# A selective-scan kernel: two PSUM banks for the scan input and two for projection tiles, and a unit's four gates in one go

## The chip, the cores and the metric

The kernel runs on one core of one Trainium2 chip. The metric is the device time of one execution in microseconds (us). One execution was also taken by the hardware profiler; all rows below come from that one.

## What is computed

Two sequences of 1024 tokens with 256 features go through two layers. The first is a state-space layer: a normalisation, then for each direction (forward and backward in time) an input projection, a scan over time, a gate and an output projection, then a gated MLP. The second is attention with 16 heads and a second MLP. The part that the change touches is the scan of the first layer, which for each of 512 channels keeps 64 states:

```python
xs, z = jnp.split(h @ in_w, 2, axis=-1)
xs = jax.nn.silu(xs)
proj = xs @ xproj_w
dt = jax.nn.softplus(proj[..., :D_INNER] + dt_bias)
Bm = proj[..., D_INNER:D_INNER + D_STATE]
Cm = proj[..., D_INNER + D_STATE:]
def step(hst, ins):
    dt_t, B_t, C_t, x_t = ins
    dA = jnp.exp(dt_t[:, :, None] * A)
    hst = hst * dA + (dt_t * x_t)[:, :, None] * B_t[:, None, :]
    y_t = jnp.einsum('bds,bs->bd', hst, C_t)
    return (hst, y_t)
...
y = jnp.swapaxes(ys, 0, 1) + xs * Dskip
return y * jax.nn.silu(z) @ out_w
```

## The kernel before, in words

The scan is cut into 8 units (`UNITS`): direction times sequence times half of the tokens (512). Units 0 to 3 run forward, 4 to 7 backward. In the even units a half starts from zero, in the odd ones it goes on from the end state of the unit before. A unit has 64 state steps (`DS`), numbered st; w counts them through all units, from 0 to 511. Each step has four tiles f = 0 to 3 of 128 channels by 512 tokens, so that there are 2048 scan tiles, numbered n = 4w + f (`U_TILES`).

Every tile goes through five engines' queues, each of which runs in the order in which its program is written; semaphores tie them together.

- ScalarE writes the decay of the tile (`act.activation(decay...)`, L950) and, for the next step, the time-major input scaled by B (`scan_input`, L933). Between steps it does `act_turns`: copies of projection tiles out of PSUM, and in steps 31 and 46 the long silu and softplus operations of the next unit.
- TensorE turns the scaled input into a PSUM bank with four instructions of 128 columns (`turn_u`, L1504 and L1507). I call this the fill of tile n. `take_u` gives the bank, 4 + n % `U_BANKS`, and first waits until the scan that read it last, n - `U_BANKS`, is done. Then, for the same f, TensorE adds the product of step w - 2 onto PSUM banks 0 to 3 (`reduce_state`, L1513, four instructions of 128 columns; `first_state`, with L1533 as well, in a unit's first step). After every odd f it does one piece of a projection for the next unit: `next(pieces, None)` issues one matmul of 512 columns (L1292), or one tile of four transposes. Fill, reduction and the piece if there is one are called a turn here.
- VectorE scans the tile out of the PSUM bank (L1198), 512 tokens in one instruction. After the four tiles of a step it does `dve_turns`. In step 1 of units 1 to 7 it also does `gate_y` (L1181) for the unit before, one gate of 128 by 512 after each of the four scans. A gate waits for the last reduction of the unit before, all four f of it, which TensorE issues in its step 1. TensorE's `first_state(w, c)`, which it issues in its step 2, waits for gate c, since it overwrites that bank.
- GpSimd multiplies the scanned tile by C (L713), two tiles in one instruction.
- SyncE loads the rows of C and the diagonals of B.

The projections are laid out by `turns` and `place_turns`: a tile with two matmuls or one group of transposes takes two steps, a tile with four matmuls three (`PIECES`). Units 1 to 6 have 8 tiles of two matmuls (xs and zs), 7 of four (dt, bc, out) and 9 of transposes (yT, bT, dtxT). Unit 0 has 16 of two (zs of unit 0, mean, sum, xs, zs), 5 of four and 5 of transposes; unit 7 has 14 of two (mean, sum, up), 4 of four and 4 of transposes. `place_tiles` gives each tile of the scan stage the one bank 4 + `U_BANKS`, and `take` makes TensorE wait until the engine that read the tile before it has done so. Before and after the scan the four banks 4 to 7 rotate over all tiles.

Of the kernel before, what the change touches and what calls it, by code (L numbers as in the profile page):

```python
# [42 lines left out]
RECIP_STEPS = (6, 7, 9, 10)  # L43
SUMS_STEP = 4
U_TILES = SCAN_TILES * NI
U_BANKS = 3
DIAGS = 1
DIAG_PAIRS = 3
FILLS = 16
# [8 lines left out]
def build(nc, t):  # L58
# [4 lines left out]
    with ctx:  # L63
# [40 lines left out]
        TB = HALF // P  # L104
# [32 lines left out]

        NORM_AT = {"ln0": (24064, 28160), "ln1": (26112, 22016), "rms0": (26624, 28672), "rms1": (26624, 28672)}
        sq = {name: cut(at, 2, C, HALF) for name, (at, _) in NORM_AT.items()}
        rstd = {name: cut(at, 4, HALF) for name, (_, at) in NORM_AT.items()}  # L140

        mask_i = cut(38912, B, L)[0:1].bitcast(I32)
# [64 lines left out]
        def tiles(name, who):  # L207
            first[name] = len(eaters)
            eaters.extend(who)

        def unit(u):

            d, r = divmod(u, B * HALVES)
            b, hi = divmod(r, HALVES)
            return d, b, hi, (1 - hi if d else hi)
# [59 lines left out]
        def pe_turn(u, st):  # L275
            return TURN[u].get(st)
# [21 lines left out]
        def dve_turns(u, st):  # L298

            step = TURN[u].get(st - 1)  # L300
            todo = [step] if step else []
            if step and step[0] == "mean":
                todo = [("centre",) + step[1:]]
            back = TURN[u].get(st - 2)
            if back and back[0] == "sum":
                todo += steps("recip scale", *back[1:])
            if u == UNITS - 1:
                return todo
            if st == SOFTPLUS_STEP + 1:
                todo.append(("softplus", u + 1))  # L310
            return todo
# [50 lines left out]
        def place_tiles(order, bank_of):  # L362

            for step in order:
                kind, *at = step
                if kind in ("mean", "square") and (at[0], at[1]) not in NEED:
                    NEED[at[0], at[1]] = last_update.get(ORDER[at[0]][at[1]], 0)
                who = {"mods": "d", "mean": "c", "sum": "a", "down": "x", "out": "x", "proj": "x" * C,
                       "xs": "a", "zs": "a", "dt": "a", "bc": "r", "bT": "a", "dtxT": "a", "yT": "a",
                       "qk": "a", "v": "a"}.get(kind, "")  # L370
                if kind == "up":
                    who = "da"[at[2] % 2 == 0]
                tiles(step, who)
                for g in range(len(banks), len(eaters)):
                    banks.append(bank_of(g))
                    before.append(holder.get(banks[g]))
                    holder[banks[g]] = ("tile", g)
                if kind == "out":
                    d, b, hi, half = unit(at[0])
                    last_update[b * HALVES + half] = eaters.count("x")  # L380
                if kind == "down":
                    last_update[ORDER[at[0]][at[1]]] = eaters.count("x")
                if kind == "proj":
                    last_update[at[0]] = eaters.count("x")

        place_tiles(START, lambda g: 4 + g % 4)
        u_before = [holder.get(4 + n) for n in range(U_BANKS)]
        for u in range(UNITS):
            for st in range(DS):
                if pe_turn(u, st):  # L390
                    place_tiles([pe_turn(u, st)], lambda g: 4 + U_BANKS)
        for n in range(U_TILES - U_BANKS, U_TILES):
            holder[4 + n % U_BANKS] = ("u", n)
        place_tiles(LATE, lambda g: 4 + g % 4)
# [9 lines left out]
        def free_bank(pe, was):  # L404

            if was is None:
                return
            kind, n = was
            if kind == "u":
                pe.wait_ge(s["scan_done"], n + 1)  # L410
                return
            name, each = FREES[eaters[n]]
            pe.wait_ge(s[name], each * eaten(n, eaters[n]))
# [6 lines left out]
        def take_u(pe, n):  # L420

            free_bank(pe, u_before[n] if n < U_BANKS else ("u", n - U_BANKS))
            return psum[:, 4 + n % U_BANKS, :]

# [21 lines left out]
        def rows_at(v, m):  # L446


            if m not in ROW_STEPS or (v % 2 and v // 2 + 1 == B * HG):
                return None  # L450
            return 1 - v % 2, (v + 1) // 2, ROW_STEPS.index(m)
# [3 lines left out]
        for v in range(BLOCKS):  # L455
            for m in range(BLOCK):
# [4 lines left out]
                if rows_at(v, m):  # L461
                    half, u, j = rows_at(v, m)
# [30 lines left out]
        def scan_at(w):  # L493

            u, st = divmod(w, DS)
            d, b, hi, half = unit(u)
            if hi:
                return SLIDE if d else 0
            return st // RING if d else SLIDE - st // RING
# [6 lines left out]
        def end_state(w, f):  # L506

            at = scan_at(w) + (0 if unit(w // DS)[0] else HALF - 1)
            return hs[:, w % RING, f, at:at + 1]
# [489 lines left out]
        def _(dve):  # L999
# [133 lines left out]
            def do(order):  # L1133

                for kind, *at in order:
                    if kind == "mods":
                        modulation(*at)
                    if kind == "centre":
                        centre(*at)
                    if kind == "recip":  # L1140
                        recip(*at)
                    if kind == "scale":
                        scale(*at)
                    if kind == "bc":
                        copy_rows(*at)
                    if kind == "softplus":
                        finish_dt(*at)
                    if kind == "decay rate":
                        negate_a()
                    if kind == "out":  # L1150
                        add_output(*at)
                    if kind == "up":
                        gate(*at)
                    if kind == "down":
                        update(*at)
                    if kind == "mask":
                        key_mask()
                    if kind == "rest":
                        rest(*at)
                    if kind == "third part":  # L1160
                        third_part(*at)
                    if kind == "ones of v":
                        ones_of_v(*at)
                    if kind == "first pass":
                        for w in range(*at):
                            score_max(w)
                            if w == SCORE_TILES - 1:
                                finish_max(0)
                    if kind == "proj":
                        add_attention(*at)  # L1170
# [7 lines left out]
            def gate_y(u, c):  # L1178

                dve.wait_ge(s["reduce_done"], NI * (u + 1) * DS)  # L1180
                dve.tensor_tensor(zsT[:, u % 2, c], psum[:, c, :], zsT[:, u % 2, c], ALU.mult)\  # L1181
                   .then_inc(s["gated"], 1)

            for u in range(UNITS):
                d, b, hi, half = unit(u)
                for st in range(DS):
                    w = u * DS + st
                    if hi:
                        dve.wait_ge(s["scan_done"], NI * (w - DS + 1))
                    rows = slice(scan_at(w), scan_at(w) + HALF)  # L1190
                    for f in range(NI):
                        n = NI * w + f
                        if w >= RING:
                            dve.wait_ge(s["reduce_done"], NI * (w - RING) + f + 1)
                        dve.wait_ge(s["decay_ready"], n + 1)
                        dve.wait_ge(s["u_full"], n + 1)
                        way = slice(None, None, -1) if d else slice(None)
                        dve.tensor_tensor_scan(hs[:, w % RING, f, rows][:, way], decay[:, w % 2, f, way],  # L1198
                                               psum[:, 4 + n % U_BANKS, way],
                                               end_state(w - DS, f) if hi else 0.0, op0=ALU.mult, op1=ALU.add)\  # L1200
                           .then_inc(s["scan_done"], 1)
                        if u and st == 1:
                            gate_y(u - 1, f)
                    do(dve_turns(u, st))
            for f in range(NI):
                gate_y(UNITS - 1, f)
# [470 lines left out]
```

## Time and profile before

| | us |
|---|---|
| median of 3 runs | 3551.79 |
| lowest and highest run | 3551.68 and 3552.13 |
| the profiled execution | 3553.52 |
| its span, first to last instruction | 3551.7 |
| mean granted TensorE clock, share of full speed | 0.975 |

The span has a short start (about 67 us), the scan (67.7 to 2726 us), and after it the MLP, the attention and the second MLP. An engine's busy share says how much of the span an instruction of it was running. Matmuls are pipelined and their ends are modelled, so their starts are the firmer numbers; scans on VectorE overlap by some hundredths, so that an interval between starts is shorter than one duration. A row of the timeline merges equal instructions that follow each other with under 0.15 us between them. An idle time in brackets stands with what ended it, which is not always what had caused it.

### The profile page before, as it was taken

How to read it: one execution, taken by the hardware profiler on the slowest of the kernel's cores; microseconds unless marked ns; L12 is line 12 of the kernel's file. 1: busy time of each engine (PE TensorE's matmuls, PEld its weight loads, DVE VectorE, ACT ScalarE, POOL GpSimd, SP SyncE). 2: the span in 40 equal slices, each digit the busy share in tenths (PEclk: the TensorE clock that was granted, in tenths of full speed). 3: DMA queues.
4: the chain of work that ended last, by engine and by line, in shares of the span. 5: the costliest groups of instructions: out<-in, count | busy, mean ns of one | idle time of the engine just before them, and what ended most of it. 6: DMA issues, size and time to landing. Idle time of an engine off the chain costs nothing.

```text
span 3551.7 us, 59805 instructions
## 1 busy us (share of the span) xinstructions
PE 3345.1 (94%) x22946; PEld 2573.6 (72%) x22946; DVE 2983.3 (84%) x2916; ACT 2910.1 (82%) x4664; POOL 2304.6 (65%) x1066
## 2 busy tenths in 40 slices
PE   8998999899989999999999899999899989999999
PEld 5888888888888888988988888888787432222244
DVE  4988999899889989988999899899997488888241
ACT  5999999999998998999999999998896327777621
POOL 1878898898888879888988888798687000000000
PEclk9999999999999999999999999999899989999999
DMA  3222222222222222222222222222111052211000
GB/s 112 72 73 64 79 70 67 61 68 68 68 69 87 66 62 66 70 63 60 79 68 63 60 68 70 59 86 68 51 62 54 17 127 35 37 19 19 1 6 18
DMA packets 192638, 214.17 MB, mean 60 GB/s; under 512 B 75585, under 2 KB 144961, under 8 KB 192097
## 3 DMA queue, kind: packets, MB, share of 16 engines
q1 hardware_dynamic: 192354, 210.36, 20.6%
q8 instruction: 182, 2.98, 0.3%
q14 instruction: 102, 0.84, 0.1%
HBM read 192.19 MB, written 18.06 MB: 59 GB/s over the span
## 4 chain that ended last, share of the span: by engine, by line
PE 67%; ACT 19%; DVE 8%; issue 3%; POOL 2%; DMA 0%; SPq 0%; DVEq 0%; ACTq 0%; POOLq 0%
PE psum L1292 17%; PE psum L1513 16%; PE psum L1507 13%; PE psum L1504 10%; ACT arena L950 8%; ACT arena L933 6%; DVE arena L1198 4%; PE psum L1600 3%; PE psum L1589 3%; PE psum L1564 2%; DVE row_max L1245 2%; POOL arena L697 1%; PE psum L1533 1%; POOL arena L713 1%; ACT L950 1%
## 5 line engine op out<-in xcount | busy, mean ns | idle before, releaser
L1198 DVE TENSOR_TENSOR_SCAN arena<-arena,psum 128x512 f32<-128x512 f32 x2048 | 2379.0, 1229 | 192.1 <-ACT arena L950 105.8
L713 POOL TENSOR_TENSOR arena<-arena 128x1024 f32<-128x1024 f32 x1024 | 2237.5, 2192 | 458.1 <-DVE arena L1198 434.7
L950 ACT ACTIVATE arena<-arena,a_neg 128x512 f32<-128x512 f32 x2048 | 1436.5, 712 | 178.1 <-PE psum L1507 176.3
L1513 PE MATMUL psum<-ident,arena 128*128 128x128 f32 x8192 | 1244.4, 275 | 1.6 <-POOL arena L713 1.6
L933 ACT ACTIVATE arena<-arena,bT 128x512 f32<-128x512 f32 x1536 | 1091.9, 711 | 0.0
L1507 PE MATMUL psum<-ident,arena 128*128 128x128 f32 x6144 | 1021.7, 276 | 0.0
L1513 PEld LDWEIGHTS psum<-ident,arena 128*128 128x128 f32 x8192 | 974.8, 143 | 2.1 <-POOL arena L713 2.1
L1504 PE MATMUL psum<-arena 128*128 128x128 f32 x4096 | 844.5, 288 | 104.4 <-DVE arena L1198 89.8
L1504 PEld LDWEIGHTS psum<-arena 128*128 128x128 f32 x4096 | 656.2, 194 | 350.5 <-issue 185.6
L1507 PEld LDWEIGHTS psum<-ident,arena 128*128 128x128 f32 x6144 | 754.9, 144 | 0.0
L1292 PE MATMUL psum<-arena 128*128 128x512 f32 x1472 | 708.0, 604 | 29.4 <-ACT arena L813 18.3
L1292 PEld LDWEIGHTS psum<-arena 128*128 128x128 f32 x1472 | 257.0, 194 | 221.6 <-issue 192.6
L1245 DVE TENSOR_REDUCE row_max<-psum 128x1 f32<-128x512 f32 x512 | 318.0, 676 | 58.0 <-PE psum L1564 56.6
L985 ACT ACTIVATE arena<-psum 128x512 f32<-128x512 f32 x512 | 273.4, 600 | 82.0 <-PE psum L1589 80.5
L736 POOL TENSOR_TENSOR arena<-skip_w 128x512 f32<-128x512 f32 x16 | 20.3, 1267 | 403.6 <-DVE skip_w L1271 403.6
L1564 PE MATMUL psum<-arena 97*128 97x512 bf16 x512 | 161.4, 393 | 20.3 <-DVE row_max L1245 16.9
L1589 PE MATMUL psum<-arena 100*128 100x512 bf16 x512 | 160.5, 387 | 4.3 <-ACT arena L985 3.2
L1589 PEld LDWEIGHTS psum<-arena 100*128 100x128 bf16 x512 | 35.9, 97 | 158.2 <-ACT arena L985 124.7
L1600 PE MATMUL psum<-arena 128*32 128x512 f32 x1024 | 136.4, 604 | 4.6 <-ACT skip_w L962 4.5
L729 POOL MEMSET arena<- 4x4096 f32 x3 | 10.7, 3579 | 184.5 <-DVE arena L1119 104.9
L1564 PEld LDWEIGHTS psum<-arena 97*128 97x128 bf16 x512 | 50.7, 99 | 100.0 <-DVE row_max L1245 46.3
L891 ACT ACTIVATE arena<-psum,b_up 128x512 f32<-128x512 f32 x32 | 22.0, 687 | 113.4 <-PE psum L1292 113.4
(117 smaller groups left out, 1079.9 us busy)
## 6 DMA issues: line engine op xcount, KB each, us to landing
arena<-bc_dram SPq DMA_DIRECT2D x256, 512.0 KB, 3.7
arena<-diag_dram SPq DMA_DIRECT2D x224, 128.0 KB, 2.1
arena<-qk_dram SPq DMA_DIRECT2D x96, 128.0 KB
diag_dram<-arena SPq DMA_DIRECT2D x32, 256.0 KB, 4.5
qk_dram<-arena SPq DMA_DIRECT2D x12, 512.0 KB, 4.9
arena<-in_x SPq DMA_DIRECT2D x4, 512.0 KB, 10.9
arena<-in_up_w SPq DMA_DIRECT2D x1, 2048.0 KB, 11.7
out_xT<-arena SPq DMA_DIRECT2D x8, 256.0 KB, 2.2
```

Of the source, the lines that this page charges most:

```text
L713: pool.tensor_tensor(out[:, :, way], h_now[:, :, way], c_row, ALU.mult)\
L933: act.activation(uT[:, w % 2, c - DIAGS], dtxT[:, u % 2, c], ACT.Copy, scale=bT[:, u % 2, c, st:st + 1])\
L950: act.activation(decay[:, w % 2, f], dt_[:, u % 2, f], ACT.Exp, scale=a_neg[:, d, f, st:st + 1])\
L985: act.activation(probs[:, w % 4, jj], psum[:, n % 3, :], ACT.Exp)\
L1198: dve.tensor_tensor_scan(hs[:, w % RING, f, rows][:, way], decay[:, w % 2, f, way], psum[:, 4 + n % U_BANKS, way], end_state(w - DS, f) if ...
L1245: dve.tensor_reduce(row_max[:, qt, j, kh:kh + 1], side_bank("scores", w), axis=AX.X, op=ALU.max)\
L1292: o = pe.matmul(dst, lhsT, rhs, start=k == 0, stop=k == len(pairs) - 1)
L1504: o = pe.matmul(dst[:, c * P:(c + 1) * P], dtxT[:, w // DS % 2, c, f * P:(f + 1) * P], diag[:, p % DIAG_PAIRS, w % 2], start=True, stop=True)
L1507: o = pe.transpose(dst[:, c * P:(c + 1) * P], uT[:, w % 2, c - DIAGS, f * P:(f + 1) * P], ident[:, :])
L1513: return pe.matmul(psum[:, c, f * P:(f + 1) * P], hs[:, w % RING, f, at:at + P], ident[:, :], is_transpose=True, start=False, stop=w % DS ...
L1564: pe.matmul(take_side(pe, "scores", w), stack[u % STACKS][0:PLAIN, 0, j, qt * P:(qt + 1) * P], stack[u % STACKS][0:PLAIN, 1, j, tok(kh)], ...
L1589: pe.matmul(psum[:, n % 3, :], stack[u % STACKS][0:ROWS, 1, j, kt * P:(kt + 1) * P], stack[u % STACKS][0:ROWS, 0, j, tok(qh)], start=True, ...
```

## The change

`U_BANKS` goes from 3 to 2, so fill n waits for scan n - 2. The tiles of projections alternate between banks 6 and 7 by their number. The four gates of a unit stand after the four scans of step 1, no longer one after each scan.

```diff
-U_BANKS = 3
+U_BANKS = 2
...
-                    place_tiles([pe_turn(u, st)], lambda g: 4 + U_BANKS)
+                    place_tiles([pe_turn(u, st)], lambda g: 4 + U_BANKS + g % 2)
...
                            .then_inc(s["scan_done"], 1)
-                        if u and st == 1:
-                            gate_y(u - 1, f)
+                    if u and st == 1:
+                        for c in range(TB):
+                            gate_y(u - 1, c)
                     do(dve_turns(u, st))
```

## Rows read from the trace of the kernel before

**Rows 1.** The page: span, busy time by engine, costliest group.
```profile
span 3551.7 us, 59805 instructions
...
PE 3345.1 (94%) x22946; PEld 2573.6 (72%) x22946; DVE 2983.3 (84%) x2916; ACT 2910.1 (82%) x4664; POOL 2304.6 (65%) x1066
...
L1198 DVE TENSOR_TENSOR_SCAN arena<-arena,psum 128x512 f32<-128x512 f32 x2048 | 2379.0, 1229 | 192.1 <-ACT arena L950 105.8
```

**Rows 2.** Busy time by window, unit 2: window, length, busy us, clock.
```profile
740.00:1064.00 324.00, 309.06 (x2457) 280.85 (x2456) 296.02 (x265) 301.50 (x477) 283.62 (x129) 0.98 0.22 67
```

**Rows 3.** Waits of the whole span: waiter, releaser, total us, times, longest.
```profile
PE psum L1292 <- ACT arena L813: 18.3, 7, 4.3
...
DVE arena L1198 <- PE psum L1507: 66.5, 121, 2.4
...
PE psum L1292 <- DVE arena L1034: 3.9, 5, 0.9
```

**Rows 4.** Timeline of VectorE: start, length, instruction, count, idle before.
```profile
910.16 6.93 DVE L1198 TENSOR_TENSOR_SCAN arena<-arena,psum 128x512 f32<-128x512 f32 x6 [4.80 <-ACT arena L950]
...
1504.22 9.12 DVE L1198 TENSOR_TENSOR_SCAN arena<-arena,psum 128x512 f32<-128x512 f32 x8 [0.50 <-ACT arena L950]
1513.84 9.12 DVE L1198 TENSOR_TENSOR_SCAN arena<-arena,psum 128x512 f32<-128x512 f32 x8 [0.50 <-ACT arena L950]
...
1585.99 2.33 DVE L1198 TENSOR_TENSOR_SCAN arena<-arena,psum 128x512 f32<-128x512 f32 x2 [0.50 <-ACT arena L950]
...
1601.27 2.33 DVE L1198 TENSOR_TENSOR_SCAN arena<-arena,psum 128x512 f32<-128x512 f32 x2 [0.50 <-ACT arena L950]
```

**Rows 5.** VectorE without a stop: an even unit, then an odd one.
```profile
1019.29 41.20 DVE L1198 TENSOR_TENSOR_SCAN arena<-arena,psum 128x512 f32<-128x512 f32 x37
...
1373.81 35.10 DVE L1198 TENSOR_TENSOR_SCAN arena<-arena,psum 128x512 f32<-128x512 f32 x30
```

**Rows 6.** TensorE's turns around one projection piece, and the scan behind it.
```profile
804.41 0.39 PE L1504 MATMUL psum<-arena 128*128 128x128 f32 x2
...
805.39 0.39 PE L1504 MATMUL psum<-arena 128*128 128x128 f32 x2
...
807.24 0.39 PE L1504 MATMUL psum<-arena 128*128 128x128 f32 x2
807.47 0.49 PE L1507 MATMUL psum<-ident,arena 128*128 128x128 f32 x3
...
808.09 2.33 DVE L1198 TENSOR_TENSOR_SCAN arena<-arena,psum 128x512 f32<-128x512 f32 x2 [0.50 <-PE psum L1507]
```

**Rows 7.** Steps 60 and 61 of unit 3: scans, and fills that wait for them.
```profile
1383.18 1.25 DVE L1198 TENSOR_TENSOR_SCAN arena<-arena,psum 128x512 f32<-128x512 f32 x1
...
1384.36 1.25 DVE L1198 TENSOR_TENSOR_SCAN arena<-arena,psum 128x512 f32<-128x512 f32 x1
...
1384.49 0.49 PE L1504 MATMUL psum<-arena 128*128 128x128 f32 x2
1384.82 0.49 PE L1507 MATMUL psum<-ident,arena 128*128 128x128 f32 x3
...
1385.66 0.49 PE L1504 MATMUL psum<-arena 128*128 128x128 f32 x2
...
1386.92 0.46 PE L1504 MATMUL psum<-arena 128*128 128x128 f32 x2
```

**Rows 8.** VectorE at unit 4's gates.
```profile
1410.99 0.69 DVE L1181 TENSOR_TENSOR arena<-psum,arena 128x512 f32<-128x512 f32 x1 [2.08 <-PE psum L1513]
...
1416.73 2.32 DVE L1198 TENSOR_TENSOR_SCAN arena<-arena,psum 128x512 f32<-128x512 f32 x2
1419.29 1.22 DVE L1198 TENSOR_TENSOR_SCAN arena<-arena,psum 128x512 f32<-128x512 f32 x1 [0.24 <-PE psum L1507]
1421.17 1.22 DVE L1198 TENSOR_TENSOR_SCAN arena<-arena,psum 128x512 f32<-128x512 f32 x1 [0.66 <-PE psum L1507]
1423.05 1.22 DVE L1198 TENSOR_TENSOR_SCAN arena<-arena,psum 128x512 f32<-128x512 f32 x1 [0.66 <-ACT arena L950]
```

**Rows 9.** Two windows: busy times, then granted clock (third number from the end).
```profile
1375.00:1400.00 25.00, 24.95 (x193) 21.62 (x192) 25.00 (x23) 23.71 (x39) 23.32 (x11) 1.00 0.23 75
...
1413.40:1416.60 3.20, 3.20 (x17) 3.20 (x16) 3.20 (x4) 1.56 (x3) 1.95 (x2) 0.50 0.00 0
```

## The prediction

> **What bounds the kernel now.** I read the page first. TensorE is busy for 94% of the span, but VectorE's scan is the costliest single group: 2048 scans of 1.23 us, 192 us idle before them [rows 1]. A share over the whole span does not say which of the two sets the pace, so I took one unit next. In unit 2's window of 324 us four engines are busy for 309, 296, 302 and 284 us [rows 2]: no engine has much room, and what counts is the order in which they hand tiles over. Then I read the timeline of VectorE beside that of TensorE, which gives two paces.
>
> VectorE's own pace, where it never stops, is 41.20 / 37 = 1.11 us a tile in an even unit and 35.10 / 30 = 1.17 us in an odd one [rows 5]. TensorE's turn without a projection piece is 0.98 us (from fill to fill), and with one matmul of 512 columns 1.85 us [rows 6]. So TensorE is faster than VectorE by 0.13 to 0.19 us in a plain turn and slower by 0.68 to 0.74 us in a turn with a piece. Where a tile of two matmuls lies on eight turns, TensorE needs 6 x 0.98 + 2 x 1.85 = 9.6 us, and VectorE shows exactly that: groups of 8 scans start 9.62 us apart with 0.50 us idle between them [rows 4], whatever releaser the rows name. Where four matmuls lie on twelve turns, it needs 8 x 0.98 + 4 x 1.85 = 15.2 us, and the trace has 15.28 [rows 4]. So most of a unit runs at TensorE's mean pace, and TensorE does not wait in it. What makes that possible is the ring of three banks: in the plain turns TensorE gets ahead by up to three tiles, and a late turn is paid from this lead. Where no pieces are left, TensorE runs into the ring's end: a fill starts 0.05 to 0.06 us after scan n - 3 has ended (1383.18 + 1.25 = 1384.43, then 1384.49; 1384.36 + 1.25 = 1385.61, then 1385.66). The fill of 1384.49 is done at 1385.31, and its scan is due only two scans after 1384.36, at 1386.70: 1.39 us in hand [rows 7].
>
> **Part 1, the ring of two.** It adds a wait: fill n for scan n - 2 in place of n - 3. What is queued behind it on TensorE is the reduction of the same turn, the piece and the next fill; who waits for those is VectorE, and for the reductions nobody soon. I work out whether VectorE then stands still. Let E be the end of scan n - 2. The fill starts at E + 0.06 and, having waited, takes 0.82 us (1384.49 to 1385.31) [rows 7], against 0.72 when it follows without a stop (807.24 to 807.96); the scan starts 0.13 to 0.14 after the fill (807.96 to 808.09) [rows 6]. That is E + 1.02. Scan n is due at E + 1.17 - 0.08 = E + 1.09 in an odd unit (the 0.08 is the overlap of two scans, 1384.43 less 1384.36 [rows 7]) and at E + 1.03 in an even one. So plain turns still hide the fill, by 0.07 and 0.01 us. For f = 0 the fill starts 0.14 after the scan's end (1386.92 against 1385.61 + 1.17 [rows 7]), which makes 1.08: hidden in an odd unit, 0.05 late in an even one, and some 0.08 with the restart. Over about 25 such tiles of an even unit, 2 us.
>
> A piece is no longer hidden. After fill n (at E + 0.06) the next fill comes 1.85 + 0.10 later, and its scan can start 0.72 + 0.14 after it: E + 2.87. It is due at E + 2 x 1.17 - 0.08 = E + 2.26 in an odd unit, E + 2.14 in an even one. VectorE stands for 0.61 or 0.73 us. The next piece comes two turns on: scans then are 0.98 + 1.85 = 2.83 apart, where two scans take 2.34 or 2.22, so each further piece of the run costs 0.50 or 0.62. The time between tiles' runs can't pay for it, since there VectorE sets the pace and a ring of two holds no lead. Hence:
>
> - two matmuls on 8 turns: 8 x 1.17 + 0.61 + 0.50 = 10.47 (odd) and 8 x 1.11 + 0.73 + 0.62 = 10.23 (even), against 9.62: +0.85 and +0.61;
> - four on 12 turns: 14.04 + 0.61 + 3 x 0.50 = 16.15 and 13.32 + 0.73 + 3 x 0.62 = 15.91, against 15.28: +0.87 and +0.63;
> - a tile of transposes: four instructions of 128 columns are half a plain turn, 0.49 us, so a scan that can start at E + 0.06 + 1.08 + 0.49 + 0.86 = E + 2.49: +0.23 and +0.35, all of it hidden now.
>
> The long silu and softplus operations stop VectorE as before (4.80 us before the scan at 910.16 [rows 4]). ScalarE's program is held to TensorE's fills, which now run up to one tile nearer to the scans, so such a stall can grow by 0 to 1.17 us; the fills before it were 0.5 us ahead at most, and I take 0.5 a unit.
>
> **Part 2, the second bank for projections.** It removes the wait of a projection tile for its predecessor's reader. In the trace hardly anything waits for that: the 18.3 us in 7 waits are for L813, the silu of the next unit's gate, whose data the bc tile needs anyway [rows 3]; of the waits for VectorE's centring 3.9 us in all are for the bank or the start [rows 3]. I take 2 us of gain in all, the bounds are 0 and 22 us. The Trainium skill's page Perfetto Trace Analysis, section Matmuls, says that independent matmul groups should rotate through banks so that reading one out overlaps the next. By that rule this half is a gain of up to those 22 us, and the trace shows that one bank already overlaps, since a tile's two or three steps leave its reader time.
>
> **Part 3, the gates in one go.** Now VectorE stops 2.08 us before the first gate with three scans of its own step behind it in its queue, and 0.24, 0.66 and 0.66 us in the next steps [rows 8]: 3.6 us. Afterwards the four scans run first, and by their end the last reduction is in, so the first gate has no wait. What is late next is step 2: TensorE's turn with `first_state` is 1.88 us (1419.29 to 1421.17 [rows 8]) and starts only when gate 0 is done; three turns come 0.46, 0.7 and 0.7 late, 1.9 us. That saves 1.7 us where the trace shows 3.6 and nothing where it is 2; I take 1.0 for each of 7 boundaries, bounds 0 and 3.6. It moves no DMA, and no other engine's queue changes.
>
> **The sum.** Units 1, 3, 5: 8 x 0.85 + 7 x 0.87 + 8 x 0.23 + 0.5 - 1.0 = 14.2 us each (the ninth tile of transposes lies in the softplus stall). Units 2, 4, 6: 8 x 0.61 + 7 x 0.63 + 8 x 0.35 + 2 + 0.5 - 1.0 = 13.6 each. Unit 0: 16 x 0.61 + 5 x 0.63 + 4 x 0.35 + 2, less 2 for pieces that lie in ScalarE's long stretches: 14.3. Unit 7: 14 x 0.85 + 4 x 0.87 + 4 x 0.23 - 1, less 1: 14.3. Together 43 + 41 + 29 = 112, less 2 for part 2: +110 us. The profiled execution took 3553.5 us with a span of 3551.7, the median of the runs is 3551.8; the span and the median agree, and I add to that: 3662 us. Nothing outside the scan changes: after it banks 4 to 7 rotate as before.
>
> **The rivals.**
>
> A: *half price.* If the pieces' stalls are shorter, because fills after a wait catch up by more than the 0.98 us turn shows or waits overlap the copies' turns, +50 us: 3602. For it: the ends of matmuls are modelled, and a fill may in truth be done sooner. Against it: 808.09 less 807.24 = 0.85 holds without the modelled end. 12 in 100.
>
> B: *the ring's loop is longer than a scan.* The plain turns have only 0.01 to 0.07 us to spare. If the loop scan, fill, scan is 0.05 us longer than read, nearly all of the 2048 tiles pay, about 0.04 each: +80 on top, 3740. For it: no row shows a fill and a scan of neighbouring tiles in such close order. Against it: each leg is read from rows. 14 in 100.
>
> C: *not slower.* TensorE is the laggard in most of the scan, so its fills could start after scan n - 2 has ended in any case, and then the third bank is idle; VectorE waits for fills only 66.5 us in all now [rows 3]. The gates would then give back up to 7 x 3.6 = 25 us and part 2 some: 3525. It decides if the fills next to pieces start later than E + 0.06 anyway. Against it: at 9.62 us for 8 tiles TensorE has no idle time, so it can keep that pace only if its six plain turns follow each other at 0.98, faster than scans end. 4 in 100.
>
> D: *the clock.* After TensorE had stopped at unit 4's gates its granted clock was 0.50, which is 1.2 GHz of 2.4 [rows 9]. If many short waits did the same, a plain turn would take twice 0.98, 0.8 more than a scan; over a tenth of the tiles that is +160 us on top, 3825. Against it: in 1375 to 1400 each fill waits for a scan and the clock is 1.00 [rows 9]. The Trainium skill, page TensorE: Matmul & The Clock Gate, section on psum-queue depth-cycling, describes such an oscillation where TensorE pauses often between groups; by that rule this change is at risk, and the row speaks against it here. 2 in 100.
>
> **The numbers.** The forecast, 3662, has 68 in 100, by itself from 3635 to 3700: the pieces' stalls could be 0.1 us off each way (some 350 pieces, 35 us) and the gates 7 to 15 us. Then A 12, B 14, C 4, D 2. The range reaches down to A and up to B: 3600 to 3740. About 0.2%, 7 us, is what a measurement of this kernel can tell from no change. Slower by more: all but C and a little of A, 0.95. Within 0.2%: 0.02. Faster: 0.03.
>
> **What would show it.** In the profile after: TensorE waits for a scan before most plain fills, VectorE's idle time before L1198 (192 us now [rows 1]) grows by about 110 us; groups of 8 scans come 10.2 to 10.5 us apart, not 9.6; four gates follow each other with no idle before the first; scans without pieces keep 1.11 and 1.17 us. If these last ones are longer, B is right. If fills start late after a scan's end although nothing is in front of them, or the groups stay at 9.6, the argument is wrong.

## The result, and the profile after

| | us |
|---|---|
| before, median of 4 runs (3551.3 to 3552.13) | 3551.73 |
| after, median of 4 runs (3676.51 to 3677.6) | 3676.95 |
| ratio, 95% interval | 1.0353, 1.0336 to 1.0369 |
| span of the profiled execution after | 3674.7 |
| mean granted TensorE clock after | 0.976 |

The change makes the kernel slower by 125 us, where 110 were forecast. The span grew by 123.0 us, and all of it lies inside the scan: its first scan starts 67.8 us after the start (before 67.7), and it ends at 2850.4 us (before 2727.4). From one unit's first scan to the next one's, units 0 to 7 are longer by 11.9, 16.0, 16.8, 17.9, 15.4, 17.7, 16.9 and 10.1 us.

The page of the kernel after: engines, then the scan, with its busy us, mean ns and idle us before it (before: [rows 1]). In this kernel the lines from the scan on carry a number higher by 0 or 1 (fill L1505 and L1508, reduction L1514, piece L1293; the gate is L1181 and the scan L1198 in both).

```profile
PE 3466.6 (94%) x22946; PEld 2591.4 (71%) x22946; DVE 3010.2 (82%) x2916; ACT 2929.7 (80%) x4664; POOL 2304.6 (63%) x1066
...
L1198 DVE TENSOR_TENSOR_SCAN arena<-arena,psum 128x512 f32<-128x512 f32 x2048 | 2404.4, 1234 | 301.5 <-PE psum L1508 161.7
```

VectorE stands before its scans for 301.5 us in place of 192.1, and the scans' busy time grew by another 25 us: scans that follow each other overlap by 0.08 us, and a scan after a stop has no such overlap. TensorE's busy time also grew, by 122 us with the same number of instructions, so that the page shows 94% both times: that share says nothing of the change.

The waits of the kernel after (waiter, releaser, total us, times, longest; before: [rows 3]):

```profile
PEld psum L1505 <- DVE arena L1198: 210.7, 464, 7.2
...
DVE arena L1198 <- PE psum L1508: 161.7, 302, 1.7
...
PE psum L1505 <- DVE arena L1198: 107.3, 58, 6.9
...
PE psum L1293 <- ACT arena L813: 13.0, 7, 3.5
```

Fills waited for scans for 195.2 us in 195 cases before (weight loads and matmuls together) and do so for 318.0 in 522 cases now. VectorE's waits for fills went from 66.5 us in 121 cases to 161.7 in 302. Most of these waits are short: 1181 of the 2048 fills start within 0.2 us of the end of the scan whose bank they take, before the change 335. The two engines now wait for each other in turn, which is what a ring that is too short looks like.

The timeline of VectorE in unit 2 (even), first where tiles of two matmuls lie, then tiles of four (start, length, instruction, count, idle before; before: [rows 4]):

```profile
870.51 6.85 DVE L1198 TENSOR_TENSOR_SCAN arena<-arena,psum 128x512 f32<-128x512 f32 x6 [0.50 <-ACT arena L950]
877.92 2.33 DVE L1198 TENSOR_TENSOR_SCAN arena<-arena,psum 128x512 f32<-128x512 f32 x2 [0.56 <-PE psum L1508]
880.76 6.85 DVE L1198 TENSOR_TENSOR_SCAN arena<-arena,psum 128x512 f32<-128x512 f32 x6 [0.50 <-ACT arena L950]
...
959.35 6.85 DVE L1198 TENSOR_TENSOR_SCAN arena<-arena,psum 128x512 f32<-128x512 f32 x6
966.76 2.33 DVE L1198 TENSOR_TENSOR_SCAN arena<-arena,psum 128x512 f32<-128x512 f32 x2 [0.56 <-PE psum L1508]
...
975.26 6.85 DVE L1198 TENSOR_TENSOR_SCAN arena<-arena,psum 128x512 f32<-128x512 f32 x6 [0.50 <-ACT arena L950]
```

A group of eight scans takes 880.76 - 870.51 = 10.25 us (forecast 10.23, before 9.62), one of twelve 975.26 - 959.35 = 15.91 (forecast 15.91, before 15.28). Each piece now shows as a stop of its own, 0.56 for a tile's first and 0.50 for the next. In unit 3 (odd) the same groups are:

```profile
1234.38 7.14 DVE L1198 TENSOR_TENSOR_SCAN arena<-arena,psum 128x512 f32<-128x512 f32 x6 [0.38 <-PE psum L1508]
...
1244.86 7.15 DVE L1198 TENSOR_TENSOR_SCAN arena<-arena,psum 128x512 f32<-128x512 f32 x6 [0.38 <-PE psum L1508]
...
1304.15 7.13 DVE L1198 TENSOR_TENSOR_SCAN arena<-arena,psum 128x512 f32<-128x512 f32 x6
...
1320.29 7.14 DVE L1198 TENSOR_TENSOR_SCAN arena<-arena,psum 128x512 f32<-128x512 f32 x6 [0.38 <-PE psum L1508]
```

That is 10.48 and 16.14 us (forecast 10.47 and 16.15). The Trainium skill, page Perfetto Trace Analysis, section Optimization Strategy, says that the same gap repeating on the engine that should be saturated can mean that there is not enough PSUM to allocate the next tile. The rows after agree. But the kernel before shows gaps of 0.50 us too [rows 4], and those come from TensorE's own work, as its turns show [rows 6]: the gap alone does not tell the two apart, the length of the group beside the sum of TensorE's turns does.

### The profile page after: what moved, and what is told of

It is laid out like the page before. It is cut to its first block, busy times and chain, and to the rows that moved or that the text cites. A ratio compares the mean times of both kernels' runs of the same rounds, so it can differ in the third digit from the quotient of the medians.

```text
span 3674.7 us, 59805 instructions
## 1 busy us (share of the span) xinstructions
PE 3466.6 (94%) x22946; PEld 2591.4 (71%) x22946; DVE 3010.2 (82%) x2916; ACT 2929.7 (80%) x4664; POOL 2304.6 (63%) x1066
## 4 chain that ended last, share of the span: by engine, by line
PE 72%; DVE 13%; ACT 9%; issue 3%; POOL 2%; DMA 0%; SPq 0%; DVEq 0%; ACTq 0%; POOLq 0%
PE psum L1514 17%; PE psum L1293 17%; PE psum L1508 14%; PE psum L1505 13%; DVE arena L1198 9%; PE psum L1601 3%; ACT arena L950 3%; PE psum L1590 3%; ACT arena L933 2%; PE psum L1565 2%; DVE row_max L1246 2%; POOL arena L697 1%; PE psum L1534 1%; POOL arena L713 1%; ACT L950 1%
## 5 line engine op out<-in xcount | busy, mean ns | idle before, releaser
L1198 DVE TENSOR_TENSOR_SCAN arena<-arena,psum 128x512 f32<-128x512 f32 x2048 | 2404.4, 1234 | 301.5 <-PE psum L1508 161.7
L1514 PE MATMUL psum<-ident,arena 128*128 128x128 f32 x8192 | 1244.4, 275 | 0.7 <-POOL arena L713 0.7
L1508 PE MATMUL psum<-ident,arena 128*128 128x128 f32 x6144 | 1021.2, 276 | 0.0
L1505 PE MATMUL psum<-arena 128*128 128x128 f32 x4096 | 908.5, 304 | 118.1 <-DVE arena L1198 107.3
L1505 PEld LDWEIGHTS psum<-arena 128*128 128x128 f32 x4096 | 651.3, 192 | 468.6 <-issue 214.5
L1514 PEld LDWEIGHTS psum<-ident,arena 128*128 128x128 f32 x8192 | 974.8, 143 | 0.9 <-POOL arena L713 0.9
L1508 PEld LDWEIGHTS psum<-ident,arena 128*128 128x128 f32 x6144 | 753.8, 143 | 0.0
L1293 PE MATMUL psum<-arena 128*128 128x512 f32 x1472 | 708.5, 604 | 23.1 <-ACT arena L813 13.0
L1293 PEld LDWEIGHTS psum<-arena 128*128 128x128 f32 x1472 | 257.9, 194 | 214.0 <-issue 191.4
L729 POOL MEMSET arena<- 4x4096 f32 x3 | 10.7, 3578 | 184.6 <-DVE arena L1119 104.8
```

The costliest lines, as they stand in the source:

```text
L1293: o = pe.matmul(dst, lhsT, rhs, start=k == 0, stop=k == len(pairs) - 1)
L1505: o = pe.matmul(dst[:, c * P:(c + 1) * P], dtxT[:, w // DS % 2, c, f * P:(f + 1) * P], diag[:, p % DIAG_PAIRS, w % 2], start=True, stop=True)
L1508: o = pe.transpose(dst[:, c * P:(c + 1) * P], uT[:, w % 2, c - DIAGS, f * P:(f + 1) * P], ident[:, :])
L1514: return pe.matmul(psum[:, c, f * P:(f + 1) * P], hs[:, w % RING, f, at:at + P], ident[:, :], is_transpose=True, start=False, stop=w % DS ...
```

## Experiments

The theory is the forecast's: the ring of two costs what TensorE's plain turns (0.98 us, faster than a scan) could bank before, and the pieces spend it. Each kernel was timed together with the kernel before on the same chip, and that one's median was 3552.4 for e1 to e4, 3552.6 for e5 to e8 and 3553.3 for e9 and e10.

**The gates alone.** The kernel before, its three banks kept, with part 3:

```diff
                             .then_inc(s["scan_done"], 1)
-                        if u and st == 1:
-                            gate_y(u - 1, f)
+                    if u and st == 1:
+                        for c in range(TB):
+                            gate_y(u - 1, c)
```

> The kernel before with part 3 alone: the ring of three and the one projection bank stay, the four gates stand after the four scans. My theory: it gives back about 1 us at each of 7 unit boundaries, 3545 us (3538 to 3549), so that parts 1 and 2 together cost 132 us. Rival: the gates' place is worth nothing by itself, because first_state in the next step is what is late: 3552.

Measured: 3551.03 us (3547.63 to 3552.63), ratio 0.9994 (0.9985 to 1.0003). VectorE at unit 4's gates in this kernel (before: [rows 8]):

```profile
1411.75 2.46 DVE L1181 TENSOR_TENSOR arena<-psum,arena 128x512 f32<-128x512 f32 x4
1414.12 2.32 DVE L1198 TENSOR_TENSOR_SCAN arena<-arena,psum 128x512 f32<-128x512 f32 x2
1416.63 1.22 DVE L1198 TENSOR_TENSOR_SCAN arena<-arena,psum 128x512 f32<-128x512 f32 x1 [0.19 <-PE psum L1508]
1418.51 1.22 DVE L1198 TENSOR_TENSOR_SCAN arena<-arena,psum 128x512 f32<-128x512 f32 x1 [0.66 <-PE psum L1508]
1420.39 4.74 DVE L1198 TENSOR_TENSOR_SCAN arena<-arena,psum 128x512 f32<-128x512 f32 x4 [0.66 <-ACT arena L950]
```

The wait of 2.08 us before the first gate is gone, as forecast. Step 1 is 1.5 to 2.2 us shorter at the seven boundaries, but step 2 is longer by 1.6 us at four of them and by 3.2 at one, since `first_state` now starts only after gate 0 and its turns of 1.88 us follow with no lead. The stop moved one step on. Steps 1 and 2 together give 4.5 us in the profiled execution, and it is lost again elsewhere: 2.7 us of it at step 50, whose length changes with the clock (below, under the long stops), 1.0 in unit 7. So the expected gain of 7 us did not come, as the rival had it for the total. Hence parts 1 and 2 carry the whole loss.

**The second projection bank alone.** The kernel after, with part 2 undone:

```diff
-                    place_tiles([pe_turn(u, st)], lambda g: 4 + U_BANKS + g % 2)
+                    place_tiles([pe_turn(u, st)], lambda g: 4 + U_BANKS)
```

> The changed kernel with projection tiles in bank 6 alone (bank 7 unused in the scan). My theory: the second projection bank hides nothing that counts, 3677 to 3680 us. Rival: it saves the waits of projection tiles, some 20 us, and without it the time is 3697.

Measured: 3677.3 us (3675.8 to 3677.75), ratio 1.0349 (1.0333 to 1.0365). One bank less, and the time is the same within 0.4 us. The second projection bank is worth nothing here, neither by itself nor to hide some of the ring's loss. The rule of the Trainium skill on rotating banks (Perfetto Trace Analysis, section Matmuls), which the prediction weighed, gave nothing in this kernel, where a tile is spread over two or three steps.

**Few pieces.** Both kernels with most of the pieces' work taken out:

```diff
                 for k, (lhsT, rhs) in enumerate(pairs):
-                    o = pe.matmul(dst, lhsT, rhs, start=k == 0, stop=k == len(pairs) - 1)
+                    if in_scan and not whole:
+                        if k < len(pairs) - 1:
+                            yield
+                            continue
+                        flat = top_parts.rearrange("p a b c -> p (a b c)")
+                        for q in range(TB):
+                            o = pe.matmul(dst[:, q * P:(q + 1) * P], ident_b[:, :], flat, start=True, stop=True)
+                    else:
+                        o = pe.matmul(dst, lhsT, rhs, start=k == 0, stop=k == len(pairs) - 1)
```

> The kernel before with nearly all of the projection pieces left out in the scan stage: of each projection tile only its last piece is issued, as four bf16 matmuls of 128 columns of constants, so the values of the first layer are not the reference's (the tiles of mean and sum stay whole). My theory: VectorE then sets the pace, odd units 322 us and even ones 307, in all about 3460 us (3440 to 3475). Rival (TensorE's mean pace doesn't bound the scan): no change beyond 20 us.

Measured: 3466.57 us (3466.53 to 3466.6), ratio 0.9756 (0.9738 to 0.9774).

> The same with the changed kernel. My theory: the ring of two costs at late turns, so with few and short pieces the difference to the kernel before with few pieces falls from 125 us to 25 to 50 us (transposes, the tiles f = 0 of even units, the turns after the long stops): about 3495. Rival (the loop scan, fill, scan is longer than a scan, every tile pays): the difference stays above 100 us, 3560 or more.

Measured: 3524.91 us (3524.21 to 3525.61), ratio 0.992 (0.9902 to 0.9938). The distance between the two is 58 us, where it is 125 with all pieces: 67 us, over half, hang on them. Rival B is out: in the ring of two VectorE runs without a stop for long once the pieces are gone, in e4:

```profile
859.36 33.05 DVE L1198 TENSOR_TENSOR_SCAN arena<-arena,psum 128x512 f32<-128x512 f32 x29
897.68 2.33 DVE L1198 TENSOR_TENSOR_SCAN arena<-arena,psum 128x512 f32<-128x512 f32 x2 [5.28 <-ACT arena L950]
```

That is 33.05 / 29 = 1.14 us a scan; steps without a piece are at most 0.1 us longer than in e3. But 58 is more than the 25 to 50 that I had expected. By steps, the rest lies at transposes (0.2 to 0.3 us each) and in the steps after a long ScalarE operation: steps 31 and 32 cost 2.8 us more in the odd units, steps 46 and 47 another 2.0 to 2.4. That is a term that the forecast had at 0.5. And of the 58 us units 0 and 7 alone take 20.8: unit 7, whose tiles of mean and sum keep their whole pieces, takes 12.5.

**The third fill after a long stop.** The kernel after shows at unit 2's silu, on VectorE:

```profile
946.16 2.33 DVE L1198 TENSOR_TENSOR_SCAN arena<-arena,psum 128x512 f32<-128x512 f32 x2 [5.10 <-ACT arena L950]
949.01 1.22 DVE L1198 TENSOR_TENSOR_SCAN arena<-arena,psum 128x512 f32<-128x512 f32 x1 [0.52 <-PE psum L1508]
950.93 1.22 DVE L1198 TENSOR_TENSOR_SCAN arena<-arena,psum 128x512 f32<-128x512 f32 x1 [0.70 <-PE psum L1508]
953.68 2.33 DVE L1198 TENSOR_TENSOR_SCAN arena<-arena,psum 128x512 f32<-128x512 f32 x2 [1.53 <-PE psum L1508]
```

and on TensorE:

```profile
944.10 1.12 PE L1293 MATMUL psum<-arena 128*128 128x512 f32 x2 [1.73 <-ACT arena L813]
...
947.44 0.80 PE L1505 MATMUL psum<-arena 128*128 128x128 f32 x2 [2.22 <-DVE arena L1198]
948.03 0.85 PE L1508 MATMUL psum<-ident,arena 128*128 128x128 f32 x3
948.67 1.06 PE L1514 MATMUL psum<-ident,arena 128*128 128x128 f32 x4
949.52 0.64 PE L1505 MATMUL psum<-arena 128*128 128x128 f32 x2
```

and in the table by window (length, then busy us of the engines, then the granted clock, third from the end):

```profile
947.40:951.40 4.00, 3.96 (x18) 3.96 (x19) 2.79 (x3) 3.54 (x6) 2.19 (x1) 0.50 0.00 0
```

Two filled banks are all the ring has. When the stop ends, the third fill has to wait for the first scan (946.16 + 1.22 = 947.38, then 947.44), and TensorE, which has stood for 1.73 us before the bc tile's first piece (944.10) and for 2.22 us behind it, is at 0.50 of its clock: the turn to the next fill takes 949.52 - 947.44 = 2.08 us where 0.98 is usual, and the bc tile's second piece (951.44) lies on top. VectorE stands for 0.52, 0.70 and 1.53 us. At full clock the third fill would just have been in time: by the prediction's legs its scan could start at 947.44 + 0.82 + 0.14 = 948.40, and the two scans before it end at 946.16 + 2.33 = 948.49. So by this sum the first two of these stops need both, a fill that has to wait and the slow clock. In the kernel before, TensorE goes on from its first piece to the third fill without waiting for a scan, still within the stop. Its rows there:

```profile
908.09 2.08 PE L1292 MATMUL psum<-arena 128*128 128x512 f32 x2 [2.54 <-ACT arena L813]
909.96 0.64 PE L1504 MATMUL psum<-arena 128*128 128x128 f32 x2
...
911.71 0.39 PE L1504 MATMUL psum<-arena 128*128 128x128 f32 x2
```

Pieces and a slow fill (909.96, its turn 1.75 us) lie before or beside the first scan at 910.16, with two filled banks in hand, and VectorE scans six tiles without a stop [rows 4]. The softplus stop shows the same without a piece. In the kernel before all three banks are full when it ends, and the refill behind the first scan (994.49 us) takes 1.44 us at half clock with two filled banks in hand: VectorE does not stop. In the kernel after, the refill (1035.94) is the one that VectorE needs third, and it stands for 0.51 and 0.70 us. To see how much of the silu's stop is the piece's, both kernels were run with the bc tile two steps later:

```diff
-SILU_STEP, SOFTPLUS_STEP, DTX_STEP = 31, 46, 48
-BC_STORE_PAIR = 18
+SILU_STEP, SOFTPLUS_STEP, DTX_STEP = 31, 48, 50
+BC_STORE_PAIR = 19
...
-                    st = max(st, SILU_STEP + 1)
+                    st = max(st, SILU_STEP + 3)
```

> The kernel before with the bc tile two steps after the silu step, no longer one, and all that follows it (dt, softplus, dtxT, the store of C) two steps later. My theory: the ring of three holds enough for the slow turns after the silu, so nothing is gained: 3552 us, 3545 to 3556.

Measured: 3566.29 us (3563.63 to 3570.23), ratio 1.0039 (1.0026 to 1.0052).

> The same with the changed kernel. My theory: after the silu stop the fill of the third tile must wait for the first scan and then runs at half clock, and the bc pieces in the same and the next step add 1.5 us of idle time a unit; two steps later they meet full clock. 7 units x 1.5 = 10 us less than the changed kernel: 3667. Rival: the surplus at the silu is ScalarE's smaller lead alone and does not depend on where the bc tile stands: 3677.

Measured: 3676.87 us (3672.06 to 3678.26), ratio 1.0347 (1.0333 to 1.0362). In e6:

```profile
948.48 1.22 DVE L1198 TENSOR_TENSOR_SCAN arena<-arena,psum 128x512 f32<-128x512 f32 x1 [0.51 <-PE psum L1508]
950.40 1.22 DVE L1198 TENSOR_TENSOR_SCAN arena<-arena,psum 128x512 f32<-128x512 f32 x1 [0.70 <-PE psum L1508]
952.03 6.85 DVE L1198 TENSOR_TENSOR_SCAN arena<-arena,psum 128x512 f32<-128x512 f32 x6 [0.41 <-PE psum L1508]
```

The stop of 1.53 us became 0.41, and steps 32 and 33 are together 1.9 to 2.4 us shorter. The total did not follow: the bc tile, begun at a usual place, pays a usual tile's price there, and the steps behind shift. So 0.51 and 0.70 a unit belong to the fills after the stop themselves, and the piece's lateness is only moved. My expectation of 10 us was wrong, and so was that of no change for e5: the kernel before became 14 us slower. From the start of the span to the end of the scan, its stretches at half clock add up to 160 us against 130. That can't be all of it: unit 2 has 10.2 us at half clock in both kernels and is still 1.3 us longer. One difference is that the bc tile's first piece lay inside the silu stop before and doesn't in e5. What each of the two costs was not tested.

**More plain turns for a tile.** One step more after every second xs and zs tile, in the kernel after (e7), and in e1's kernel, three banks and gates in one go (e8):

```diff
-SILU_STEP, SOFTPLUS_STEP, DTX_STEP = 31, 46, 48
-BC_STORE_PAIR = 18
+SILU_STEP, SOFTPLUS_STEP, DTX_STEP = 35, 50, 52
+BC_STORE_PAIR = 20
...
+                if 0 < u < UNITS - 1 and step[0] in ("xs", "zs") and step[2] % 2:
+                    st += 1
```

> The changed kernel with one more step without pieces after every second xs and zs tile in units 0 to 5 of the next unit's work (4 steps in all, taken from the steps without pieces at a unit's end; silu, bc, dt, softplus and dtxT come 4 steps later). My theory: a ring of two holds no lead between pieces, so their spacing is worth nothing: 3677 us, 3672 to 3681. Rival: it is TensorE's mean pace that bounds, and wider spacing saves 0.5 us for each added step of an even unit and 0.2 of an odd one, 10 us: 3667.

Measured: 3672.78 us (3669.89 to 3676.95), ratio 1.0342 (1.0326 to 1.0358).

> The same spacing with the ring of three, one projection bank and the gates in one go. My theory: here the mean pace of TensorE does bound, so the spacing saves those 10 us: 3541 us (3536 to 3547). If it comes out at 3551, the lead of three tiles is too short to carry over the added step.

Measured: 3539.65 us (3535.23 to 3542.05), ratio 0.9962 (0.995 to 0.9975). The same edit gives 11 us with three banks (3551.03 to 3539.65). With two it is 4 (3676.95 to 3672.78), which can't be told from nothing: the intervals of the two ratios overlap (1.0336 to 1.0369 and 1.0326 to 1.0358). By units the profiles say the same: units 2, 4 and 6 are shorter by 2.9, 3.2 and 3.0 us with three banks and by 0.9, 0.2 and 1.6 with two. In e8 (its scan is L1200) twenty scans follow each other where the kernel before stops after eight:

```profile
849.19 9.12 DVE L1200 TENSOR_TENSOR_SCAN arena<-arena,psum 128x512 f32<-128x512 f32 x8
858.80 22.69 DVE L1200 TENSOR_TENSOR_SCAN arena<-arena,psum 128x512 f32<-128x512 f32 x20 [0.50 <-ACT arena L952]
```

So an added plain step pays where the ring can bank its lead. This kernel, e8, is 13 us faster than the kernel before and the fastest of all here that do the whole work.

**Smaller pieces.** Both kernels with each projection matmul of the scan cut in two of 256 columns, one in every turn in place of a whole one in every second:

```diff
+                if in_scan:
+                    for k, (lhsT, rhs) in enumerate(pairs):
+                        for half in range(2):
+                            cols = slice(half * HALF // 2, (half + 1) * HALF // 2)
+                            o = pe.matmul(dst[:, cols], lhsT, rhs[:, cols], start=k == 0 and half == 0,
+                                          stop=k == len(pairs) - 1 and half == 1)
...
-                    if f % 2:
-                        next(pieces, None)
+                    next(pieces, None)
```

> The kernel before with every projection matmul of the scan stage cut into two of 256 columns, one after each turn in place of one of 512 after every second turn (transposes stay after odd f). TensorE has the same columns to do and twice the weight loads for them. My theory: with the ring of three the mean counts, so nothing is gained and the extra loads cost 0 to 35 us: 3552 to 3587.

Measured: 3575.46 us (3575.08 to 3576.51), ratio 1.0063 (1.004 to 1.0086). Cutting the pieces costs 22 us by itself.

> The same with the changed kernel. My theory: a turn late by 0.43 us costs the ring of two less than half of a turn late by 0.86 us, since each turn has 0.2 us to spare against the scan; by the sum of the prediction 0.2 us less for a tile of two matmuls and 0.23 for one of four, some 25 us in all. So the distance to the kernel before with half pieces is about 100 us, not 125. Rival (the cost goes by the columns that TensorE has to do, not by how late one turn is): the distance stays at 125.

Measured: 3664.96 us (3661.96 to 3667.96), ratio 1.0314 (1.0284 to 1.0344). Unit 2 of e10 (the reduction and fills carry other numbers there):

```profile
854.51 1.22 DVE L1198 TENSOR_TENSOR_SCAN arena<-arena,psum 128x512 f32<-128x512 f32 x1 [0.19 <-PE psum L1523]
855.93 1.22 DVE L1198 TENSOR_TENSOR_SCAN arena<-arena,psum 128x512 f32<-128x512 f32 x1 [0.20 <-PE psum L1523]
...
859.13 5.73 DVE L1198 TENSOR_TENSOR_SCAN arena<-arena,psum 128x512 f32<-128x512 f32 x5
...
869.31 5.73 DVE L1198 TENSOR_TENSOR_SCAN arena<-arena,psum 128x512 f32<-128x512 f32 x5 [0.20 <-PE psum L1523]
```

A turn with a half piece is 1.42 us (855.93 - 854.51), and a tile's eight scans take 869.31 - 859.13 = 10.18. The four turns without a piece take what is left, (10.18 - 4 x 1.42) / 4 = 1.13 us, VectorE's pace. This gives the loss a simple form, found after the results. With whole pieces three turns of the eight hold or touch the two pieces, and five plain ones lose what they could bank: 5 x (1.11 - 0.98) = 0.65 (measured 10.25 - 9.62 = 0.63), in an odd unit 5 x (1.17 - 0.98) = 0.95 (measured 0.86). With half pieces four plain turns are left: 4 x 0.13 = 0.52. The kernel e9 has 859.54 to 869.17 = 9.63 for the same eight, so the loss there is 0.55:

```profile
859.54 8.01 DVE L1198 TENSOR_TENSOR_SCAN arena<-arena,psum 128x512 f32<-128x512 f32 x7 [0.20 <-PE psum L1522]
...
869.17 8.01 DVE L1198 TENSOR_TENSOR_SCAN arena<-arena,psum 128x512 f32<-128x512 f32 x7 [0.20 <-PE psum L1522]
```

In all, e10 and e9 are 89.5 us apart (e10 with only two runs, 6 us from each other), where the expectation said 100 and its rival 125: the rival is out, and the saving was larger than expected. In units 1 to 6 of the profiled executions the ring's price is 82.3 us with half pieces and 100.8 with whole ones, 18.5 less. Another 8.5 lies in unit 7, where e9 by itself is 10.7 us longer than the kernel before; why was not looked into.

**What can't be run.** A ring of two with the gates as before would close a circle. Gate 0 waits for the last reduction of the unit before, which stands behind step 1's fill of f = 3 on TensorE; with two banks that fill waits for the scan of f = 1, and this one stands behind gate 0 on VectorE. With three banks the fill waits for the scan of f = 0, ahead of the gate. So part 3 is not an option beside part 1 but what it needs, which the prediction didn't say. It follows from the order of the programs; no run shows it.

## Why the prediction was right, point by point

**The pace.** Right. The argument that TensorE banks a lead in plain turns and spends it on pieces gave all four groups to 0.02 us, and e7 with e8, and e9 with e10, move as it says. The rivals that touch it fell: A (half price) by the groups' lengths, B (every tile pays) by e4, C (not slower) by the result itself. Plain steps of an even unit take 4.52 us against 4.44, which is the 0.08 for f = 0, and those of an odd unit keep 4.69. (By its own legs the prediction's 1.08 for that fill is 0.14 + 0.82 + 0.14 = 1.10; the term it led to was measured as forecast.)

**The transposes.** 0.20 and 0.25 us, not 0.23 and 0.35: even units were 0.8 over.

**The long stops.** The step that was mis-sized. The prediction gave the silu and softplus 0.5 us a unit, because "the fills before it were 0.5 us ahead at most". That covers only how much longer the stop itself gets, and there it holds: 5.10 us against 4.80 at the silu of unit 2, no change at the softplus (7.10 both times). What comes behind the stop was put at nothing. Measured, steps 31 to 33 cost 2.8 to 3.8 us more in units 1 to 6, 1.1 to 1.4 of them forecast for stop and tile; step 47 costs 1.3 to 1.4 more. What I left out: before, the third bank was filled ahead of the first scan; and the fill behind these stops is done at half clock.

Step 50 gives 1.3 to 1.5 us back in units 1, 3 and 5, and that is the clock. TensorE waits there for a product of GpSimd, 2.0 to 2.2 us in the kernel before and 0.7 to 1.0 after. Before, the step takes 7.2 to 7.6 us in four of seven units, where the mean granted clock over it is 0.77 to 0.78, and 6.1 in the three others, where it is 1.00 with a wait of the same length. After, it takes 5.6 to 6.0 in all seven, at 1.00. So what the change seems to give back at this step depends on how the clock fell in the one profiled execution of the kernel before. Over units 1 to 6 the surplus at steps 31 to 33 is 13.0 us, step 47 adds 8.2, step 50 takes back 4.7: 16.5 us.

**The gates.** Forecast -1.0 a boundary. Where no pieces are in the way (e4 against e3) step 1 is 1.2 to 1.6 us shorter at each of seven boundaries and step 2 longer by 1.6 at three of them, which is 9.8 less 4.8, or -0.7 each. Between the kernels before and after, steps 1 and 2 are together 5.8 us shorter over the seven boundaries: 2.2 at unit 4, where the kernel before had its 3.6 us of stops, 1.1 at unit 7, and 0.2 to 0.6 at the five others, where it has no stop in step 2 but the change brings one. The prediction had weighed both cases, 1.7 and nothing. With three banks (e1) it is -0.5 at a boundary with both effects, and in all nothing that the measurement tells from none. The stop in step 2 was named in the prediction as what is late next, and the trace shows it with that size (0.18, 0.66 and 0.66 in unit 2):

```profile
787.16 2.46 DVE L1181 TENSOR_TENSOR arena<-psum,arena 128x512 f32<-128x512 f32 x4
789.54 2.32 DVE L1198 TENSOR_TENSOR_SCAN arena<-arena,psum 128x512 f32<-128x512 f32 x2
792.04 1.22 DVE L1198 TENSOR_TENSOR_SCAN arena<-arena,psum 128x512 f32<-128x512 f32 x1 [0.18 <-PE psum L1508]
793.93 1.22 DVE L1198 TENSOR_TENSOR_SCAN arena<-arena,psum 128x512 f32<-128x512 f32 x1 [0.66 <-PE psum L1508]
795.81 39.39 DVE L1198 TENSOR_TENSOR_SCAN arena<-arena,psum 128x512 f32<-128x512 f32 x34 [0.66 <-ACT arena L950]
```

**The second bank.** Forecast -2, measured 0 (e2). Of the 18.3 us of waits for the silu 13.0 are still there: it is a wait for data.

**The ends.** Units 0 and 7 were forecast at 14.3 each and came to 11.9 and 10.1: I had taken off 2 and 1 us for pieces that lie in ScalarE's long stretches. In unit 0, step 50 alone is 1.9 shorter, by the clock as above. In unit 7 steps 26 to 31 go up and down by 0.5 to 1.4 us and nearly cancel; which piece lies beside what was not counted, so this part is left open.

**The sum.** Units 1 to 6 came to 100.8 us, forecast 83.4: 17.4 short, nearly all of it the 16.5 at the long stops. Units 0 and 7 came to 22.0, forecast 28.6: 6.6 over. With the 2 of the second bank that leaves 12.9 (before rounding), which is 122.9 less 110. That the forecast stands no more than 15 us from the measured time is in part luck, since errors of opposite sign add up in it; the largest term, the pieces, is right by itself.

**The clock.** Rival D did not occur: the mean is 0.976 (before 0.975), the stretches at half clock inside the scan add up to 124 us in both kernels, and short waits leave the clock alone in the window of unit 2 that holds the groups above:

```profile
868.00:893.00 25.00, 25.00 (x187) 21.35 (x187) 22.38 (x20) 22.52 (x37) 21.03 (x10) 1.00 0.16 59
```

The oscillation from cycling through PSUM banks that the Trainium skill describes (TensorE: Matmul & The Clock Gate, psum-queue depth-cycling) is thus not seen in these stretches.

## What to carry to other kernels

Where a producer's mean turn is about the consumer's pace but its turns are uneven, the depth of the ring between them is worth, as here, the sum of what its short turns could bank, not a fixed handover time: write down the loop (end of use, refill, start of use) and the long turn, and compare both with one and with two periods. Before giving a buffer from such a ring to another user, look at what waits for that user now: here 22 us at most were to be had, and 0 came, for 125 lost. And check an order of work that was written for the deeper ring, since a shorter one can close a circle.

## What the runs showed that was not expected

The restart of TensorE after a long stop costs twice its usual time. In 947.4 to 951.4 us the granted clock was 0.50, that is 1.2 of 2.4 GHz, after TensorE had stood for 1.73 and, behind a single piece, for 2.22 us; a plain turn took 2.08 and then 1.92 us (to the piece at 951.44) against 0.98. With three banks such slow turns lay within the stop or beside its first scan (908.09 to 911.71). The same waits of 2.0 to 2.2 us at step 50 of the kernel before were followed by half clock in four units and by full clock in three. And moving the bc tile and what follows it by two steps made the kernel before 14 us slower (e5), more than the whole gain that was to be had there: places in this schedule interact over many steps, and a change of a few us a unit can't be read off one stretch.
